# Edge convolutions of a graph network: each gather of turn i waits for an event of TensorE in turn i - 1 in place of turn i - 2

## The reference, cut to what matters

```python
def _egnn_conv(x, src, dst, edge_attr, W_msg, W_edge, W_root, b):
    msg = x[src] @ W_msg + edge_attr @ W_edge
    agg = jax.ops.segment_max(msg, dst, num_segments=x.shape[0])
    agg = jnp.where(jnp.isneginf(agg), 0.0, agg)
    return agg + x @ W_root + b
c1 = jax.nn.leaky_relu(_egnn_conv(X, src, dst, edge_attr, W1_msg, W1_edge, W1_root, b1))
c2 = jax.nn.leaky_relu(_egnn_conv(c1, src, dst, edge_attr, W2_msg, W2_edge, W2_root, b2))
```

## Time and profile before

| what | us |
| --- | --- |
| median of 3 runs (lowest to highest) | 2287.12 (2282.48 to 2293.44) |
| the profiled execution | 2304.43 |
| its span, from the first to the last instruction | 2302.6 |
| PE busy in the span | 2030.8 (88%) |
| DVE busy | 1240.7 (54%) |
| POOL busy | 759.0 (33%) |
| ACT busy | 672.1 (29%) |

### The profile page before, as it was taken

How to read it: one execution, slowest core, us unless ns; L and a number is a source line. 1 busy time by engine, 2 the same in 40 slices (tenths; PEclk the granted TensorE clock), 3 DMA queues, 4 the chain that set the end, 5 groups by cost and what they waited for, 6 DMA issues and landing times. The chain is left out here.

```text
span 2302.6 us, 57334 instructions
## 1 busy us (share of the span) xinstructions
PE 2030.8 (88%) x23524; PEld 1924.2 (84%) x23524; DVE 1240.7 (54%) x3485; ACT 672.1 (29%) x1939; POOL 759.0 (33%) x762
## 2 busy tenths in 40 slices
PE   4599688888888678888888699999999999999998
PEld 4499578777777567777777599999999999999988
DVE  8946366566565446666656474444444444444635
ACT  6824122222221212222222133332333333333434
POOL 2567366666555266656566510000000000000000
PEclk9999899999999789999999899999999999999999
DMA  3054445545554435555455400000000000000000
GB/s 75 1 164 131 106 123 137 132 132 132 131 133 117 122 87 134 134 131 133 130 132 130 126 17 2 2 2 2 2 2 2 2 2 2 1 2 2 2 2 23
DMA packets 153147, 163.58 MB, mean 71 GB/s; under 512 B 43697, under 2 KB 141612, under 8 KB 152885
## 3 DMA queue, kind: packets, MB, share of 16 engines
q1 hardware_dynamic: 100493, 83.89, 14.3%
q0 software_dynamic: 20464, 32.18, 7.5%
q10 hardware_dynamic: 31928, 43.84, 5.3%
HBM read 100.90 MB, written 58.89 MB: 69 GB/s over the span
## 5 line engine op out<-in xcount | busy, mean ns | idle before, releaser
L1473 PE MATMUL c_taken<-rows,conv_hot 125*128 125x192 f16 x6500 | 639.2, 253 | 102.7 <-issue 92.3
L1423 POOL DMA_INDIRECT conv_rows<-messages,idx_all x572 | 578.3, 1011 | 411.7 <-issue 121.6
L1473 PEld LDWEIGHTS c_taken<-rows,conv_hot 125*128 125x128 f16 x6500 | 555.7, 101 | 153.2 <-issue 137.3
L1540 DVE TENSOR_SCALAR conv_hot<-head_offset_srcs 125x640 f16<-125x640 f16 x1300 | 346.3, 328 | 272.2 <-DMA c_mask<-segment_mask 90.5
L1726 PE MATMUL l_ps<-rows,counts 125*128 125x192 f16 x5625 | 466.2, 246 | 1.9 <-DVE rows L1830 1.9
L1726 PEld LDWEIGHTS l_ps<-rows,counts 125*128 125x128 f16 x5625 | 464.0, 98 | 2.4 <-DVE rows L1830 2.4
L1726 PE MATMUL l_ps<-conv_rows,counts 125*128 125x192 f16 x5000 | 414.0, 246 | 0.8 <-DVE conv_rows L1871 0.8
L1726 PEld LDWEIGHTS l_ps<-conv_rows,counts 125*128 125x128 f16 x5000 | 412.6, 98 | 1.0 <-DVE conv_rows L1871 1.0
L1550 DVE TENSOR_TENSOR_SCAN c_scanned<-c_mask,c_scanned,c_msg 96x512 f32<-96x512 bf16 x208 | 264.5, 1272 | 151.0 <-DMA c_need<-deg 55.3
L1862 DVE SCALAR_TENSOR_TENSOR l_uf<-l_ps,l_cf,l_wide 125x96 f32<-125x96 f32 x400 | 127.1, 318 | 317.6 <-ACT l_wide L1797 317.6
L1603 ACT ACTIVATE c_back<-c_tr 128x384 f32<-128x384 f32 x208 | 102.0, 491 | 536.0 <-PE c_tr L1500 180.6
(11 more groups left out here) (297 smaller groups left out, 1774.3 us busy)
## 6 DMA issues: line engine op xcount, KB each, us to landing
running_max<-c_back ACTq DMA_DIRECT2D x208, 192.0 KB
c_attr<-attr_halves SPq DMA_DIRECT2D x412, 64.0 KB
c_mask<-segment_mask SPq DMA_DIRECT2D x206, 96.0 KB
conv_rows<-messages,idx_all POOLq DMA_INDIRECT x572
head_srcs<-sources SPq DMA_DIRECT2D x50, 160.0 KB
l0a_raw<-in_ea_t SPq DMA_DIRECT2D x50, 132.8 KB, 2.3
attr_halves<-l0a_hi SPq DMA_DIRECT2D x50, 66.4 KB, 2.1
attr_halves<-l0a_lo SPq DMA_DIRECT2D x50, 66.4 KB, 2.1
```

What stands on the lines that cost most here:

```text
L1423: pool.indirect_dma_start(out=gat[:, i % 2, j, :], out_offset=None, in_=c["y_d"], in_offset=bass.IndirectOffsetOnAxis(ap=idx_all[:, i * IT ...
L1473: return pe.matmul(acc[:, (NB * i + j // 2) % ACCS, j % 2 * (2 * F):(j % 2 + 1) * (2 * F)], hot[:, slot + k, j * ET:(j + 1) * ET], y[:, t, :],
L1540: last = v.tensor_scalar(hot[:, SLOTS[h % len(SLOTS)] + k, :], off[:, :], float(t * P - SRC_MID), None, ALU.is_equal)
```

## The change

The second semaphore wait ahead of each gather of the turns from 2 on names an event one turn later. Nothing else is changed: the same number of instructions in the same order on every engine, the same DMAs, the same buffers. With the new argument gathers of turn i + 1 are issued in TensorE's turn i. The wait on `s_msg` stays, and is now always met when it is reached at a later turn's event.

```diff
                             if i >= 2:
                                 if j % GT == 0:
                                     pool.wait_ge(s_msg, (i - 1) * GT + g + 1)
-                                room(i - 2, j)
+                                room(i - 1, j)
                             pool.indirect_dma_start(
```

## The result

The changed kernel takes 2300.47 us (median of 10, 2295.88 to 2305.43), the kernel before beside it 2287.22 (median of 10, 2278.87 to 2297.0). The ratio is 1.0061 [1.0044, 1.0078]: 13.3 us slower, the 0.5% line just crossed. Forecast were +7.4 us and 2294.5.

The account below looks back on a forecast made before the run. TensorE was taken to set the time, held up by unbroken rows of POOL's gathers. Per convolution -3.2 (turn 0), -6.5 (turn 24), +13.4 (tail) make +3.7, twice +7.4: from 2287.1 to 2294.5 us, 8-in-10 range 2280 to 2309.

Parts of the forecast that it names:

- Turn 0: First turn of a convolution: loses its gathers and falls from 18.4 to 15.2 us, a gain of 3.2 us a convolution.
- turn 24: Carries next turn's gathers instead of 11 unbroken result gathers: 24.9 to 18.4 us, a gain of 6.5 us a convolution.
- The body: Turns 1 to 23: same gather cadence, so unchanged at 18.4 and 18.5 us a turn; cost 0.
- The rival of late rows: In the body, one turn in three loses 1 us to a late gather: +8 a convolution, 2310 us; chance 0.05.
- The tail: Turn 25 to the block's end: 22 result gathers delay the next phase from 18.9 to 32.3 us, losing 13.4 a convolution.
- nothing but POOL's own rate sets it: In the tail, awaited events are long past, so result gathers run at POOL's 1.25 us each, row ending at 31.8 us.
- one of the prediction's own signs of being wrong: At the end of a convolution's block: the forecast is wrong if the block closes before POOL's row of gathers ends.
- This rival: In the tail, 22 unbroken gathers hold TensorE to their end: +3.2 more a convolution, +13.8 in all, 2301 us; chance 0.14.
- Its own sign: At the block's end: the rival of TensorE held to the row's end holds if TensorE's drain ends behind POOL's last gather.
- The second rival: Gathers don't make turns long, so turns 0 and 24 gain nothing: +26.8, 2314 us; whole or half, chance 0.14.
- The rest: All that follows the two convolutions: taken as unchanged, with no term in the sum.
- POOL doesn't close the block: At the block's end the next phase starts when the chain is done; tail stays 18.9: -19.4, 2268 us; chance 0.05.

Follow-up runs that it names:

- no_body_gathers: The kernel before with the gathers of turns 2 to 25 left out (output not the reference's): 2096.32 us on the first kind of chip.
- paced_results: The kernel before, with the first 11 early result gathers each also waiting for an event of turn 24: 2275.22 us, ratio 0.9971, first kind of chip.
- paced_15: `paced_results` with 15 early result gathers in place of 22: 2036.6 us, ratio 0.9988, second kind of chip.
- the sliding order: `paced_results` with the gathers of turns 1 to 25 spread evenly over earlier turns' events: ratios 1.0019 and 0.9996, second kind of chip.
- after: The changed kernel itself, in its first profile on the first kind of chip: median 2300.47 us, ratio 1.0061.

## Why the prediction was right, and where it wasn't

*Turn 0, turn 24.* Forecast -6.4 and -13.0 for both convolutions, measured -5.4 and -13.3. For turn 24 the step is confirmed by `no_body_gathers` and `paced_results`: gathers hold TensorE up, and a row without a pause does it more than the body's pace. For turn 0 the size was luck. The step took 18.4 us for it though the earlier trace rows show 15.2 for that very turn; the first convolution gained 0.7 us there and the second, where the turn had taken 20.5 and 21.0 us, 4.6. Nor were 15.2 and 14.9 the cost of a turn free of hold-ups: turn 0 had 8 gathers in it and turn 10 had 9, single turns of before run from 14.9 to 23.6 us, and without gathers it is 14.3.

*The body.* Its cost was put at 0. The sum of the turns grew on neither kind of chip (832 us against 842 on the first, 14.3 us a turn in before and after on the second), and no wait for rows shows, so rows came in time. The rival of late rows is out.

*The tail.* +26.8 forecast, +27.2 measured, but "nothing but POOL's own rate sets it" is the step that failed, and one of the prediction's own signs of being wrong came true: the block closed at 767.4, before POOL's row ended at 769.2. POOL's row was no unbroken one: it stopped after 15 gathers, for 4.46 us, because gathers 16 to 19 wait for `messages(25, 1)`, which the forecast called long past. TensorE, with 58 matmuls to do, was held under the row of gathers, and its chain closed the block. This rival had been worked out from the end of an unbroken row, 3.7 us behind it, and was given 2301. Its own sign didn't come: TensorE's drain took 0.9 us and ended near 766.1, not behind the last gather, which starts at 768.28. In fact POOL's last gather of the unbroken part ended at 756.3, and 3.6 us later the scan could start: it looks as if the row, blocked by the chain that it held up, set it free by pausing. The same 3.6 to 3.7 us stand behind the pause in all four profiled tails, though it came behind 19 gathers in one and 15 in the others. That is argued from the rows; no run took that wait away. On the second kind the same 58 matmuls under the same gathers had ScalarE at the meeting 10.4 us behind the first message of turn 25 (635.1 - 624.7), against 31.6 here, so the hold-up itself is shown. That the tail landed near the forecast's value is a coincidence of two lengths. TensorE's early end in the records, marked as such in the forecast by its drain, was the right hint. The Trainium skill's Perfetto Trace Analysis, section "Summary: the profiler window per engine type", calls the end of a TensorE window an estimate; in this trace the readers of a group go on 22 us behind it.

*The second rival.* On the first kind of chip it is wrong. On the second it is right: a turn takes 14.3 us with its gathers, as long as a turn without them on the first kind. The Trainium skill, DMA: Bandwidth & Descriptors, section "Queues, rings and completion order", has each DMA engine serve its queues by turns, and these traces agree with it. But the rival's price, 13.4 us a tail, is wrong even there. It is 5, for two reasons: the sequencer passes the meeting 14.5 us ahead of its engine, and POOL ran so late before that its row moved by 5 us only.

*The rest.* +9.5 us forecast at 0. This term wasn't in the sum at all. Taken off the +13.3 of the medians it leaves near +4, below the 0.5% line. The stages a change doesn't touch were taken as fixed, which they are not when a granted clock differs in them.

*POOL doesn't close the block (the rival on the fast side).* Its premise came true on the first kind of chip, its time did not: with POOL out of it, the chain that takes its place is late by as much.

## What to carry to other kernels

When work is moved ahead by a turn, follow what is queued behind it on the same in-order engine to the loop's end: there the space that it leaves is filled at once by a row without gaps, and on the first kind of chip it was TensorE that paid. The better edit was the opposite one, to leave the gathers where they are and spread the row behind them (0.9971 on one kind of chip; on the other only `paced_15` and the sliding order have it, and they show no clear difference). And before a difference of half a per cent is explained by stages, profile both kernels more than once: one stage that nobody touched moved by 9.5 us here, and turns 1 to 23 of the same kernel by 14.

## What the hardware showed that was not expected

- One program, two kinds of chip: 2282 to 2287 us, and 2036 to 2037 on two others. The gap is in the two convolutions. With the body's gathers left out, the first kind reaches 14.31 us a turn as well, so it is TensorE beside indirect gathers that differs. The largest entry of TensorE's waits in `after`, on the first kind, is the takes, 93 us in 186 pieces with nothing that the profile shows as their reason (total, times, longest):

```profile
PE c_taken L1473 <- issue: 93.0, 186, 2.5
```

  Through what a gather holds TensorE on the one and not on the other stays open; DMA engines were 53% busy in these turns on the first kind and 65% on the second, which has no hold-ups.
- At the end of a block POOL's sequencer was through with its gathers 14.5 us before its engine (640.0 against 654.5, where the last gather starts at 653.6). The meeting at a block's end counts the sequencer; the next phase starts with POOL's engine still at work.
- TensorE's record of a group stood 22 us ahead of the moment at which the engines that waited for it went on.
